# A GRU scan beside an RK4 scan: the GRU's state in two halves of its column tiles, 24 gate pairs behind each of the four stages, and the square of the new q on ScalarE

## The reference

```python
# block 1: GRU over time, h of (4, 512)
gi = x_t @ W_ih + b_ih ; gh = h @ W_hh + b_hh        # r, z, n parts of 512 columns each
r = sigmoid(i_r + h_r) ; z = sigmoid(i_z + h_z)
n = tanh(i_n + r * h_n) ; h = (1 - z) * n + z * h     # x_t + h is the second block's drive

# block 2: FitzHugh-Nagumo, one RK4 step (DT = 0.01) per time step, q and p of (4, 512)
def slope(q, p): 
    dq = q - q**3 / 3 - p + drive_t + tanh(q) @ coupling.T + bias
    dp = 0.08 * (q + 0.7 - 0.8 * p)
dq1 = slope(q, p); dq2 = slope(q + DT/2 dq1, ..); dq3 = slope(q + DT/2 dq2, ..); dq4 = slope(q + DT dq3, ..)
q = clip(q + DT/6 (dq1 + 2 dq2 + 2 dq3 + dq4), -20, 20)     # p likewise
```

## Time and profile before

| | |
|---|---|
| median of 3 runs | 3735.89 us (3733.82 to 3738.52) |
| the profiled execution: its time, its span | 3739.69 us, 3737.9 us |
| PE, DVE, ACT, POOL busy | 89%, 76%, 64%, 35% |
| mean granted TensorE clock | 0.958 |
| the two scans | about 208 to 3597 us of the span |
| of the chain that ended last | PE 63%, DVE 24%, issue 6%, ACT 6% |

### The profile page before, as it was taken

One profiled execution on the slowest core, in us unless ns is written; L12 is line 12 of the kernel. 1 busy time (PEld: TensorE's weight loads), 2 busy tenths in 40 slices (PEclk: granted clock), 3 DMA queues, 4 the chain that ended last, 5 costly groups with the idle time before them and its releaser, 6 DMA issues.

```text
span 3737.9 us, 289917 instructions
## 1 busy us (share of the span) xinstructions
PE 3339.9 (89%) x115469; PEld 3127.5 (84%) x115469; DVE 2823.8 (76%) x18140; ACT 2387.9 (64%) x20639; POOL 1300.2 (35%) x5145
## 2 busy tenths in 40 slices
PE   8989899999998899899989899999889899999878
PEld 4478888888888888888888888888888888888854
DVE  2068777777778778777777777787777777787766
ACT  3256666666666666666666666666666666666653
POOL 0023333333333333333333333333333333333321
PEclk9999999999999999999999999999999999999978
DMA  3000000000000000000000000000000000000001
GB/s 124 23 24 1 1 1 1 1 1 1 1 1 1 1 1 1 1 1 1 1 1 1 1 1 1 1 1 1 1 1 1 1 1 1 1 1 1 1 1 45
DMA packets 9382, 23.85 MB, mean 6 GB/s; under 512 B 556, under 2 KB 600, under 8 KB 8792
## 3 DMA queue, kind: packets, MB, share of 16 engines
q1 hardware_dynamic: 8832, 19.92, 1.4%
q10 hardware_dynamic: 88, 0.02, 0.0%
HBM read 15.75 MB, written 4.19 MB: 5 GB/s over the span
## 4 chain that ended last, share of the span: by engine, by line
PE 63%; DVE 24%; issue 6%; ACT 6%; DVEq 0%; DMA 0%; ACTq 0%; POOL 0%
PE psum L1093 36%; PE psum L1073 21%; DVE qnext L832 5%; PE psum L1045 4%; DVE tpart L789 4%; ACT cand L475 3%; DVE psum L832 3%; DVE gates L733 3%; DVE narg L744 2%; DVE psum L825 1%; DVE h L765 1%; PE psum L1194 1%; ACT tpart L528 1%; DVE zdiff L757 1%; DVE gated L739 1%
## 5 line engine op out<-in xcount | busy, mean ns | idle before, releaser
L1093 PE MATMUL psum<-tpart,cpl 128*128 128x32 f16 x65536 | 2012.7, 177 | 339.4 <-DVE tpart L789 332.8
L1093 PEld LDWEIGHTS psum<-tpart,cpl 128*128 128x128 f16 x65536 | 1824.1, 96 | 404.0 <-DVE tpart L789 395.6
L1073 PE MATMUL psum<-hpart,whh 128*128 128x32 f16 x49152 | 1479.1, 177 | 7.8 <-DVE hpart L720 7.6
L1073 PEld LDWEIGHTS psum<-hpart,whh 128*128 128x128 f16 x49152 | 1354.4, 96 | 9.5 <-issue 6.2
L528 ACT ACTIVATE tpart<-psum 128x8 f16<-128x8 f32 x3072 | 519.0, 174 | 516.3 <-DVE psum L832 447.9
L789 DVE SCALAR_TENSOR_TENSOR tpart<-tfull,tpart 128x8 f16<-128x8 f32 x4096 | 667.2, 165 | 167.7 <-ACT tfull L530 97.2
L832 DVE TENSOR_REDUCE psum<-psum 128x8 f32<-128x24 f32 x3072 | 561.3, 191 | 182.5 <-PE psum L1093 7.4
L530 ACT ACTIVATE tfull<-psum 128x8 f32<-128x8 f32 x3072 | 513.4, 172 | 0.0
L341 POOL TENSOR_TENSOR uhat<-uscaled,bhat 128x16 f32<-128x16 f32 x512 | 113.3, 221 | 1105.3 <-ACT uscaled L516 1105.3
L499 ACT ACTIVATE qterm<-psum 128x16 f32<-128x16 f32 x3072 | 428.2, 213 | 0.0
L813 DVE SCALAR_TENSOR_TENSOR psum<-sq,psum 128x16 f32<-128x16 f32 x1536 | 274.9, 179 | 182.1 <-ACT qterm L499 113.6
(11 more groups left out here) (151 smaller groups left out, 3553.9 us busy)
## 6 DMA issues: line engine op xcount, KB each, us to landing
xrow<-in_x_dram SPq DMA_DIRECT2D x4, 1024.0 KB, 11.4
out_dram<-space SPq DMA_DIRECT2D x16, 256.0 KB, 2.0
wih<-in_L_cond_W_ih_dram SPq DMA_DIRECT2D x3, 1024.0 KB, 10.1
space<-in_L_cond_W_hh_dram SPq DMA_DIRECT2D x1, 3072.0 KB, 18.7
space<-in_L_cond_coupling_dram SPq DMA_DIRECT2D x1, 1024.0 KB, 19.4
xrow<-in_cond_dram SPq DMA_DIRECT2D x1, 1024.0 KB, 4.5
wih<-in_L_cond_Wk_dram SPq DMA_DIRECT2D x1, 1024.0 KB, 5.3
wih<-in_L_cond_Wo_dram SPq DMA_DIRECT2D x1, 1024.0 KB, 7.6
```

Of the source, the lines that this page charges most:

```text
L1073: mm = pe.matmul(gate_out[part][:, :, :, col:col + B], whh[:, w, k, n * P:(n + 1) * P], copies_in(hpart[:, k, :, :]), start=(col == 0 and ...
L1093: mm = pe.matmul(stage_out[a][:, :, :, col:col + B], cpl[:, w, k, n * P:(n + 1) * P], copies_in(tpart[:, s % 2, k, :, :]), start=(col == 0 ...
```

## The change

- **The GRU's state in halves.** All gates of the column tiles of half a (n, r, z: six products' columns, 24 columns of sums) are made and used apart from those of half b: one sum of 24 columns (`sum_gates`), one sigmoid over r and z, then `reset`, `argument`, `candidate`, `weigh`, `new_h`, `h_low` on 8 columns each.
- **Where its matmuls stand.** 24 behind each stage: the second half of h times half of the gates of a, and more, behind stage 0 (`gates_finish_a`), the rest of b behind stage 1 (`gates_finish_b`), and the next GRU step's first 48 behind stages 2 and 3 (`gates_start_a`, `gates_start_b`).
- **The new h.** `h = (1 - z) n + z h` is made as `fresh + kept`: ACT makes `omz` = (1 - z) with the scale of h (two operands that are a column of a tile, `bias=scale[:, 2:3]`, `scale=kap[:, 5:6]`), DVE `fresh = omz * cand`, POOL `kept = z * hs`. The high part of h is written by DVE straight from that sum; `hs` is the scaled h, and ACT makes the plain h from it at the end of a step (`plain_h`).
- **The order on ACT and DVE.** `stage_terms(0)` and `(1)` stand behind the cubic term of DVE (`cub_ready`), in stage 0 behind `sigmoids(0)` too; `sum_stage` of stages 1 and 2 now waits for them (`qterm_ready[s]`), which `cubic` did before. `gate_input` moves from stage 1 to the end of the step.
- **The square.** ACT squares `qnext` behind the tanh of stage 3 (`sq[:, 0]`); DVE limits it and adds the constant (`shift_square`), and `clip` makes `q1` alone.

The pieces below are, from the top, the orders of the gates, a helper of POOL, one of ACT, ACT's step, two helpers of DVE, and PE's step.

```diff
-GATE_ORDER = list(range(2 * K, 3 * K)) + list(range(0, 2 * K))
-GATES_AFTER = [range(0, K), range(K, 2 * K), range(2 * K, G3), range(0)]
+GATES = [[2 * K + n for n in half] + [n for n in half] + [K + n for n in half]
+         for half in (range(0, HK), range(HK, K))]
...
+            def keep_part(x, v):
...
+                pool.tensor_tensor(kept[:, x, :], rz[:, x, HC:2 * HC], hs[:, (v - 1) % 2, x * HC:(x + 1) * HC],
+                                   ALU.mult).then_inc(kept_ready[x], 1)
...
+            def sigmoids(x, v):
+
+                act.wait_ge(gate_sum[x], v)
+                act.activation(rz[:, x, :], gates[:, x, HC:HG], ACT.Sigmoid, scale=k_gate).then_inc(rz_ready[x], 1)
+                act.wait_ge(rz_ready[x], v)
+                act.activation(omz[:, x, :], rz[:, x, HC:2 * HC], ACT.Identity, bias=scale[:, 2:3],
+                               scale=kap[:, 5:6]).then_inc(omz_ready[x], 1)
...
+                        if s == 1 and a == 0 and gru <= T:
+                            candidate(0, gru)
...
+                    if s == 0:
+                        if gru <= T:
+                            sigmoids(0, gru)
+                        act.wait_ge(cub_ready, stage_count(1, now))
+                        stage_terms(0)
+                    if s == 1:
+                        if tail <= T:
+                            scaled_drive(tail)
+                        act.wait_ge(cub_ready, stage_count(2, now))
+                        stage_terms(1)
+                        if gru <= T:
+                            sigmoids(1, gru)
+                    if s == 2 and gru <= T:
+                        candidate(1, gru)
                     if s == 3:
-                        if gru < T:
-                            h_high(gru + 1, gru)
                         if tail <= T:
                             first_terms(tail)
...
+                        if gru <= T:
+                            plain_h(gru)
+                        if gru < T:
+                            gate_input(gru + 1)
...
             def sum_stage(s, a, v):
 
-                dve.wait_ge(base_ready[s], v)
+                dve.wait_ge(base_ready, stage_count(s, v))
                 dve.wait_ge(stage_mm[s][a], v)
+                if a == 0 and s in (1, 2):
+                    dve.wait_ge(qterm_ready[s], v)
...
+            def shift_square(v):
+
+                dve.wait_ge(sq_ready[0], v - 1)
+                dve.tensor_scalar(square0, sq[:, 0, :], CLAMP * CLAMP, LINEAR[0], ALU.min, ALU.add).then_inc(shift_ready, 1)
...
-            def step(now, gru):
+            def step(now, begun, following):
                 for s in range(4):
...
+                    if s == 0 and begun:
+                        gates_finish_a()
+                    if s == 1 and begun:
+                        gates_finish_b()
+                    if s == 2 and following is not None:
+                        gates_start_a(following)
+                    if s == 3 and following is not None:
+                        gates_start_b(following)
```

More of the change, by code:

```diff
@@ L379, in step @@
                     if s == 1 and tail <= T:
-                        next_drive(tail, now)
+                        next_x1(tail, now)
+                    if s == 1 and gru <= T:
+                        keep_part(1, gru)
+                    if s == 1 and tail <= T:
+                        next_uhat(tail)
                 if tail <= T:
@@ new lines, in plain_h @@
+            def plain_h(v):
+                for x in range(HALVES):
+                    act.wait_ge(hs_ready[x], v)
+                if v > 1:
+                    act.wait_ge(x1_ready, v - 1)
+                act.activation(h[:, :], hs[:, v % 2, :], ACT.Copy, scale=k_unh).then_inc(h_ready, 1)
+            for v in (1, 2):
+                gate_input(v)
+                sigmoids(0, v)
+                sigmoids(1, v)
+                candidate(0, v)
+                candidate(1, v)
+                plain_h(v)
@@ L489, in _ @@
+            gate_input(3)
             first = condT[:, :, :].rearrange("p k b -> p (k b)")
@@ new lines, in weigh, with new_h @@
+            def weigh(x, v):
+                dve.wait_ge(omz_ready[x], v)
+                dve.wait_ge(cand_ready[x], v)
+                dve.tensor_tensor(fresh[:, x, :], omz[:, x, :], cand[:, x, :], ALU.mult).then_inc(fresh_ready[x], 1)
+            def new_h(x, v):
+                dve.wait_ge(kept_ready[x], v)
+                dve.wait_ge(fresh_ready[x], v)
+                if v < T:
+                    if x == 0:
+                        dve.wait_ge(ka_read, v)
+                    dve.tensor_tensor(part_of(x, 0), in_k(fresh[:, x, :]), in_k(kept[:, x, :]),
+                                      ALU.add).then_inc(hi_ready[x], 1)
+                if v > 2:
+                    dve.wait_ge(h_ready, v - 2)
+                dve.tensor_tensor(hs_of(x, v), fresh[:, x, :], kept[:, x, :], ALU.add).then_inc(hs_ready[x], 1)
@@ L771, in _ @@
                 link(ins)
+            for x in range(HALVES):
+                dve.tensor_copy(part_of(x, 0), in_k(hs_of(x, 0))).then_inc(hi_ready[x], 1)
+                h_low(x, 0)
             for v in (1, 2):
-                h_high(v)
-                h_low(v)
-                sum_nr(v)
-                reset(v)
-                argument(v)
-                difference(v)
-                sum_z(v)
-                weigh(v)
-                new_h(v, v - 1 if v > 1 else None)
-                dve.wait_ge(h_ready, v)
-            h_high(3)
-            h_low(3)
+                for x in range(HALVES):
+                    sum_gates(x, v)
+                for x in range(HALVES):
+                    reset(x, v)
+                    argument(x, v)
+                for x in range(HALVES):
+                    weigh(x, v)
+                    new_h(x, v)
+                    h_low(x, v)
             def split_tanh(s, a, v, ready, n):
@@ L866, in step @@
                 base(1, now)
+                if gated_step:
+                    reset(0, gru)
+                    argument(0, gru)
                 sum_stage(1, 0, now)
@@ L886, in step @@
                 if gated_step:
-                    difference(gru)
-                    sum_z(gru)
+                    weigh(1, gru)
                 base(3, now)
+                if gated_step:
+                    new_h(1, gru)
                 sum_stage(3, 0, now)
-                if gated_step:
-                    weigh(gru)
+                if gru < T:
+                    h_low(1, gru)
                 sum_stage(3, 1, now)
-                if gated_step:
-                    new_h(gru)
                 if tail <= T:
@@ L900, in step @@
                     split_tanh(0, 1, tail, tanh_ready[3][1], now)
-                    square(tail)
-                    if gru < T:
-                        h_low(gru + 1)
+                    shift_square(tail)
                     cubic(0, tail)
@@ new lines, in gate_products @@
+            def gate_products(x, cs, ks):
+                for c in cs:
+                    n = GATES[x][c]
+                    for k in ks:
+                        for w in range(2):
+                            mm = pe.matmul(gate_out[x][:, :, :, c * B:(c + 1) * B], whh[:, w, k, n * P:(n + 1) * P],
+                                           copies_in(hpart[:, k, :, :]), start=(c == 0 and k == 0 and w == 0),
+                                           stop=(c == len(GATES[x]) - 1 and k == K - 1 and w == 1), skip_group_check=True)
+                return mm
```

289 lines of the change are left out of this document (137 added, 152 removed).

## The result

| | before | after |
|---|---|---|
| median | 3737.2 us (3733.82 to 3740.4) | 3932.38 us (3930.42 to 3937.42) |
| ratio | | 1.0524, 95% 1.0506 to 1.0543 |
| span of the profiled execution | 3737.9 us | 3935.6 us |
| mean granted TensorE clock | 0.958 | 0.984 |

The kernel is slower by 195 us. The forecast was 3869 us (3660 to 3945), and slower with a chance of 0.74: the side is right, the size was put at 133.

What follows compares the result with a forecast made beforehand. PE was taken to bound stages 0 to 2, the chain stage 3; +0.04 + 0.16 + 0.09 + 0.01 = +0.30 us a step over 510 steps, +153 us less 20, gave 3869 us, range 3660 to 3945.

Steps and rivals of the forecast that it cites:

- Stage 1, the main term: Stage 1's first sum waits for ACT's terms, behind `omz`, until 1.06 after the first product: 1.78 us, +0.16.
- The price of a column operand: On ACT, the two column operands of `omz` hold the queue 0.20 more: 0.107 + 0.20 = 0.31 us.
- The rival in which such operands do not hold ACT: On ACT, `omz` holds the queue only 0.107, so the kernel gets faster, 3665 us; chance 0.16.
- Stage 2: `omz` of half b stands right ahead of stage 2's tanh and delays it: 1.70 us, +0.09.
- Stage 3: `weigh` at 0.41 stands ahead of the base, last `new_h` 0.70, sum at 0.80: 1.58 us, +0.01.
- the halves of h come in time: On PE, the order of its waits costs nothing, as the halves of h come with about 0.1 us to spare.
- Stage 0: `plain_h` and `gate_input` in ACT's queue put the tanh at 1.26, where it stood at 1.21: 1.76 us, +0.04.
- PE's alone: In the kernel before, stages 0 to 2, with 32 own and 32 gate matmuls each, are bound by PE.
- What is given back: PE, no longer the bound, hides some of the 0.10 of slower or late matmuls: 0.04 a step, 20 us.
- DVE's queues: DVE gets 40 instructions a step for 35, halves of h come late: +0.15 a step more, 3945 us; chance 0.07.
- the 0.05 a stage: If TensorE's clock fell in the scan, the chain's products lengthen each stage by 0.05: +100 us, 3970; chance 0.05.
- the signs that the prediction named: In the timeline after: stages near 1.76, 1.78, 1.70, 1.58; PE idle in all four; `omz` about 0.4 long, 0.3 to next start.

Runs made afterwards that it cites:

- e1: The changed kernel with 1 - z made by POOL ahead of `kept`, not by ACT: 3754.62 us, ratio to before 1.0063.
- e5: The changed kernel with the scale of `omz` in a register, so one column operand for two: 3848.51 us, ratio to before 1.031.
- e10: e9 with `new_h(1)` behind the first sum of stage 3, not ahead of it: 3821.02 us, ratio to before 1.0235.
- e11: e9 with `plain_h` and `gate_input` moved out of ACT's queue of stage 0: 3708.9 us, ratio to before 0.9929.
- e7: The kernel before with only the square moved to ACT and one clip less on DVE: 3689.41 us, ratio to before 0.9868.
- e2: The changed kernel with the terms of stages 0 and 1 first on ACT and DVE's cubic waiting for them; `omz` stays on ACT: 3834.52 us, ratio 1.0278.
- e3: The changed kernel with both the edits of e1 and e2: 3838.85 us, ratio to before 1.0269.
- e9: e1 with the terms first on ACT in stage 1 only, stage 0 in the changed kernel's order: 3745.03 us, ratio to before 1.0027.
- e12: e11 with half b's `argument` ahead of the split that opens stage 3 and its candidate ahead of the square: 3627.2 us, ratio to before 0.9704.
- e4: The changed kernel without products of the low part of the GRU's weights, 12 gate matmuls a stage for 24: 3924.81 us, ratio 1.052.

## Why the prediction was right, and where its size was off

By its own steps, for plain steps (forecast, measured; the measured ones are medians, of stages 0 and 3 where the turn of PE's loop does not fall):

- **Stage 1, the main term: 1.78, 1.84.** The mechanism was as told, and e1 shows it by taking it away. The forecast's pieces after the split, 0.08 to the gates' sum, 0.255 to the sigmoid, 0.24 to `omz`, 0.31 to the terms, were measured as 0.10, 0.26, 0.25 and 0.30. The term that was mis-sized is the last, from the terms' start to the sum: 0.36 + 0.03 = 0.39 forecast, 2006.48 - 2006.04 = 0.44 measured. The hand-over to the sum, which waits for three semaphores, took 0.13 from the end of the terms (2006.35), not the 0.03 that I had read from a sigmoid, which waits for one.
- **The price of a column operand** was right: 0.31 forecast, 0.30 measured, and e5 confirms the half of it. The rival in which such operands do not hold ACT is refuted.
- **Stage 2: 1.70, 1.74.** `omz` of half b right ahead of the tanh: 2008.18, 2008.48. The gates' sum came at 0.44 after the first product, not at 0.39, because `new_h` waits for `fresh` to be written.
- **Stage 3: 1.58, 1.67.** This is the largest error. `weigh` was forecast at 0.41 and stands at 0.43; but from there the sum takes until 0.90, not 0.80. I counted the instructions behind it at 0.10 each; the base came 0.13 behind and `new_h` another 0.18, since it waits for what `weigh` writes. The statement that the halves of h come in time "with about 0.1 us to spare" is true of after, but thin: e10 moved `h_low` by 0.14, and PE waited.
- **Stage 0: 1.76, 1.70**, too high by 0.06. The cost of the longer ACT queue is there (e11 wins 0.09 by clearing it); but the square's move gains on its own 0.06 (e7, 1.73 to 1.67), which I had set at nothing because ACT, not the base, would hold the tanh. In e7 the tanh came 0.07 sooner with the base. How much of the gain is alive in after was not tried apart. e7 also shows that stage 0 of the kernel before was not PE's alone, as the prediction has it: it got shorter by 0.06 with PE's work as it was.
- **What is given back: 0.04, 0.04** (mean over plain step 0.10 before, 7.01 - 6.95 = 0.06 after).

The sum was put at +0.30 and measured as +0.43 between plain steps (6.95 - 6.52); the four errors, +0.06, +0.04, +0.09 and -0.06, make the 0.13. Of the rivals, DVE's queues were given 0.07 as a small extra; e2, e3 and e9 to e12 show that they stand right behind ACT in stages 1 to 3, and that is why e1 alone didn't fall below the kernel before. The clock stayed up (0.984); e4, with half of the gates' products, shows 0.02 and 0.07 at the two sums of stage 0 from its fall and nothing lost in the time, so the 0.05 a stage that I took looks too high for a chain that waits for ACT.

Of the signs that the prediction named, the first sum of stage 1 behind ACT's terms, `omz` at 0.39 with 0.30 to the next start, and the tanh of stage 2 right behind `omz` are there. In the step shown, PE's idle brackets stand ahead of stages 2 and 3 only (0.28 and 0.17), not ahead of all four.

## What to carry to other kernels

When a small instruction is put into a queue that a chain waits on, count its column operands: on ACT one held the next instruction back by 0.09 us, about as much as a whole small instruction does (0.107). When one queue is relieved, read at once which queue gives the next last wait (here DVE's order, then PE's wait for `h_low`); the same two moves cost 38 us behind one order and won 36 behind another. When a small instruction of DVE grows in some of its steps, look at what POOL does at that time. And time each part of a change alone: the square gained 1.3%, and the halves, with 1 - z on POOL and three orders mended, are part of a version that is 3% faster than before.
